# Weighted sums of two score blocks issued together in two attention layers; one layer's values by way of DRAM

## The reference, cut to what matters

```python
# causal: 16 heads of 8, 128 keys a sequence
scores = jnp.einsum('bhqd,bhkd->bhqk', q, k) * scale + alibi_bias_causal
attn = jax.nn.softmax(scores, axis=-1)
out = einsum('bhqk,bhkd->bqhd', attn, v) @ Wo.T + bo
# rotary: 16 heads of 8, 77 context rows a sequence
q, k = apply_rope(rms_norm(x @ Wq.T)), apply_rope(rms_norm(context @ Wk.T))
attn = softmax(q k^T * D ** -0.5)
out = einsum('bhts,bhsd->bthd', attn, context @ Wv.T) @ Wo.T
x = layernorm(x + out)
```

## Time and profile before

| | |
|---|---|
| median of 3 runs | 2769.44 us (2767.96 to 2771.38) |
| profiled execution | 2773.75 us |
| its span, first to last instruction | 2772.0 us |
| PE, DVE, ACT, POOL busy | 91%, 69%, 60%, 61% of the span |
| causal stage, about | 1302 to 1827 us of the span |
| rotary stage, about | 1827 to 2420 us of the span |
| L1140 transposes, both stages | x1024 each |
| L1040 sums, both stages | x2048 records each |

### The profile page before, as it was taken

The page is one execution under the profiler, slowest core; times in us unless marked ns, Lnnn a source line. Parts: engine busy times, 40 slices in busy tenths (PEclk is TensorE's granted clock), DMA queues, the critical chain, the costliest instruction groups (busy, mean ns, idle before and its releaser), DMA issues. The chain is left out here.

```text
span 2772.0 us, 61590 instructions
## 1 busy us (share of the span) xinstructions
PE 2534.0 (91%) x19168; PEld 1864.5 (67%) x19168; DVE 1904.9 (69%) x5298; ACT 1671.0 (60%) x4543; POOL 1694.9 (61%) x2110
## 2 busy tenths in 40 slices
PE   8998999999999289996999999969999999699996
PEld 6665887877877289993555555547766666458993
DVE  6884677787777355555777777765788886445655
ACT  6773666666665234444766666639888887623334
POOL 3442334555555645554888888846688887724675
PEclk9998999999999699998999999979999999899998
DMA  8932467777774122214100000000011010011336
GB/s 260 338 107 68 151 215 226 234 224 224 223 220 129 54 65 71 72 58 129 58 11 9 9 11 9 7 25 13 16 30 30 30 30 17 30 30 54 93 93 194
DMA packets 274799, 267.86 MB, mean 97 GB/s; under 512 B 30060, under 2 KB 253561, under 8 KB 274096
## 3 DMA queue, kind: packets, MB, share of 16 engines
q1 hardware_dynamic: 256912, 228.42, 27.2%
q0 software_dynamic: 17280, 34.13, 3.6%
q10 hardware_dynamic: 288, 1.38, 0.2%
HBM read 101.24 MB, written 151.85 MB: 91 GB/s over the span
## 5 line engine op out<-in xcount | busy, mean ns | idle before, releaser
L779 POOL TENSOR_TENSOR wide_probs<-wide_exps,wide_inv_sum 128x616 f32<-128x616 f32 x128 | 168.3, 1315 | 305.6 <-DVE wide_inv_sum L1580 293.0
L749 POOL TENSOR_TENSOR causal_exps<-causal_biased,causal_neg_max 128x512 f32<-128x512 f32 x256 | 262.8, 1036 | 76.4 <-DVE causal_neg_max L1594 76.2
L758 POOL DMA_INDIRECT sorted_x<-send,place_i x240 | 244.1, 1017 | 84.2 <-ACT send L1233 44.0
L1289 ACT ACTIVATE rotary_exps<-banks,rotary_neg_max 128x77 f32<-128x77 f32 x1024 | 248.7, 341 | 19.3 <-DVE rotary_neg_max L1594 19.1
L1764 POOL DMA_INDIRECT results<-gelu_tile_out,gelu_dest_i x142 | 140.1, 986 | 142.2 <-DVE gelu_tile_out L1920 120.0
L1539 DVE TENSOR_TENSOR causal_biased<-banks,regions 128x512 f32<-128x512 f32 x256 | 163.6, 680 | 80.7 <-PE banks L1115 80.4
L1764 POOL DMA_INDIRECT results<-swiglu_tile_out,swiglu_dest_i x142 | 144.6, 1019 | 116.7 <-DVE swiglu_tile_out L1915 59.4
L1833 ACT ACTIVATE gelu_hidden<-banks,gelu_slot 128x256 f32<-128x256 f32 x284 | 116.6, 470 | 159.5 <-PE banks L2010 159.4
L1258 ACT ACTIVATE causal_exps<-causal_exps 128x512 f32<-128x512 f32 x256 | 161.2, 630 | 71.4 <-POOL causal_exps L749 71.4
L1594 DVE TENSOR_REDUCE rotary_neg_max<-banks 128x4 f32<-128x308 f32 x256 | 121.7, 475 | 113.5 <-PE banks L1129 105.1
L1273 ACT ACTIVATE causal_probsT<-banks 128x512 f32<-128x512 f32 x256 | 151.6, 592 | 79.3 <-PE banks L1140 79.3
(11 more groups left out here) (385 smaller groups left out, 7018.3 us busy)
## 6 DMA issues: line engine op xcount, KB each, us to landing
v_dram<-wide_staged SPq DMA_DIRECT2D x38, 1024.0 KB, 4.4
sorted_x<-blank SPq DMA_DIRECT2D x1, 34848.0 KB, 116.8
sorted_x<-blank SPq DMA_DIRECT2D x24, 1452.0 KB, 8.7
wide_folded<-v_dram SPq DMA_DIRECT2D x128, 256.0 KB
gelu_tile_in<-sorted_x SPq DMA_DIRECT2D x71, 132.0 KB, 2.1
swiglu_tile_in<-sorted_x SPq DMA_DIRECT2D x71, 132.0 KB, 2.1
gelu_back<-results SPq DMA_DIRECT2D x16, 512.0 KB, 8.0
swiglu_back<-results SPq DMA_DIRECT2D x16, 512.0 KB, 5.4
```

The costliest lines, as they stand in the source:

```text
L749: pool.tensor_tensor(exps[:, (NU * pair.c + m) % ES], biased[:, m % BS].rearrange("p (h n) -> p h n", h=HU), neg_max[:, m % SLOTS].unsquee ...
L758: pool.indirect_dma_start(route["sorted_x"], bass.IndirectOffsetOnAxis(ap=r_place_i[:, b % 2, which, n // 2:n // 2 + 1], axis=0), send[:, ...
L779: pool.tensor_tensor(probs[:, half % SLOTS, 0:HH * NK].rearrange("p (k h) -> p h k", h=HH), exps[:, half % EB], inv_sum[:, half % SLOTS].u ...
L1289: last = act.activation(exps[:, (NU * c.c + k) % ES, h], scores[:, h * NK:(h + 1) * NK], ACT.Exp, bias=neg_max[:, k % SLOTS, h:h + 1])
```

## The change

Three things change; the wide stage is left as it was.

1. In causal, `late_sums` replaces `late_sum`: at every even k it issues the sums of two slots together, ahead of that slot's transposes, with PLAG 5 in place of 4 and four `probsT` buffers in place of two.
2. In causal, the output's way is moved: `turn_back` and `divide` from k = 4 and 6 to 5 and 6, the values' projection from k = 3 to 4, `turn_outputs` from k = 7 to k = 1 of the next step, ACT's copy from k = 0 to 2, `project_late` from k = 1 to 3 (with it the sum and statistics on DVE from 2 to 4 and the root on POOL from 3 to 5), the residual on POOL from k = 3 to 6, the norm on DVE from k = 5, 6 to 6, 7.
3. In rotary the exponentials of eight heads (two slots) are written densely, 616 columns of 77 behind one another, padded to five blocks of 128. Two transposes at the even slot and three at the odd one turn them; ACT copies 128 x 256 and 128 x 384. `dense_sum` multiplies at odd slots only: each 32-column strip holds two heads that lie in two neighbouring blocks, so 4 strips x 2 blocks = 8 matmuls (16 records) for two slots, over all 128 rows. The values must lie in the same order: ACT writes them to `v_rows` (one buffer), SP stores them with four DMAs a pair to DRAM, and loads them back five pairs behind its first role with five DMAs a pair into `v_dense`, which has two buffers. The values' projection moves from f to e (k = 7, four steps earlier), so the lead steps have it too, and ACT's copy waits until the pair before has been stored. The context ring shrinks from 8 to 4 pairs.

```diff
-    FU = {"wide": 7, "causal": 4, "rotary": 2}[kind]
+    FU = {"wide": 7, "causal": 4, "rotary": 1}[kind]
-    EARLY = 2
+    EARLY = 3
-    OT, OT_LAG = (1, 1) if kind == "causal" else (2, 0)
+    OT, OT_LAG = (1, 3) if kind == "causal" else (2, 0)
+            def store_values(pair):
+                sp.wait_ge(early_done, pair.count(EARLY, EARLY))
+                rows = ...
+                for h in range(4):
+                    sp.dma_start(rows[h], v_rows[0:NK].rearrange("k (m r) -> k m r", r=PITCH)[:, :, 64 * h:64 * h + 64]
+                                 ).then_inc(v_stored, 16)
+            def load_values(pair):
+                sp.wait_ge(v_stored, 16 * 4 * (pair.c + 1))
+                if pair.c >= 2:
+                    sp.wait_ge(pv_done, pair.back(2).count(NU, NU))
...
+            def step(f, ahead=None, pair=None, *behind):
                 if f is not None:
                     load(f)
+                if kind == "rotary" and pair is not None:
+                    store_values(pair)
+                if kind == "rotary" and behind[2] is not None:
...
+                    load_values(behind[2])
+                    if kind == "rotary" and f.c >= CTX:
+                        sp.wait_ge(early_done, f.back(CTX).count(EARLY, EARLY))
...
+            if m == 4:
+                if f.c >= 1:
+                    act.wait_ge(v_stored, 16 * 4 * f.c)
+                return act.activation(v_rows[0:NK]...[:, :, 0:D], chip.banks[0:NK, 6, 0:2 * P]..., copy)
-                    "causal": [(0, 0), (1, 0), (2, 0), (3, 1)], "rotary": [(5, 0), (7, 0)]}[kind]
-        EARLY_AT = [(0, 0), (1, 0)]
-        TLAG, PLAG, OLAG = {"wide": (4, 5, 6), "causal": (3, 4, 5), "rotary": (2, 3, 4)}[kind]
+                    "causal": [(0, 0), (1, 0), (2, 0), (4, 1)], "rotary": [(5, 0)]}[kind]
+        EARLY_AT = [(0, 0), (1, 0), (7, 0)]
+        TLAG, PLAG, OLAG = {"wide": (4, 5, 6), "causal": (3, 5, 5), "rotary": (2, 3, 4)}[kind]
+        DIVIDE_AT = (5, 6) if kind == "causal" else (4, 6)
...
+            def late_sums(pair, n):
+                b, g = n // UB, n % UB // 2
+                pe.wait_ge(probsT_done, pair.count(NU, n + 1))
...
+                for odd in range(2):
+                    for h in range(HU):
+                        strip = 272 * 2 * b + 256 * odd + 32 * (4 * g + h)
+                        last = pe.matmul(o_bank[b][32 * h:32 * h + 32, g * P:(g + 1) * P], values[:, pair.c % 2, strip:strip + 32],
+                                         probsT[:, (n - 1 + odd) % 4, h * P:(h + 1) * P], start=odd == 0, stop=odd == 1)
+                last.then_inc(pv_done, 2)
+            def dense_sum(pair, n):
...
+                    pe.wait_ge(v_loaded[s], 16 * 5 * (pair.c // 2 + 1))
+                for second in range(2):
+                    for strip in range(4):
+                        chunk = strip + second
+                        last = pe.matmul(o_bank[b][32 * strip:32 * strip + 32, g * P:(g + 1) * P],
+                                         v_dense[:, s, b, g, chunk, 32 * (strip % 2):32 * (strip % 2) + 32],
+                                         probsT[:, (NU * pair.c + n) // 2 % 2, chunk * P:(chunk + 1) * P], start=second == 0, stop=second == 1)
+                    if kind == "causal" and at is not None and k % 2 == 0:
+                        late_sums(*at)
+                            for m in range(3 if n % 2 else 2):
+                                at = (2 * (n % 2) + m) * P
+                                last = pe.transpose(p_bank[n % 2][:, m * P:(m + 1) * P], exps[:, (NU * pair.c + n) // 2 % 2, at:at + P], ident)
+                            start, columns = 2 * (n % 2) * P, (3 if n % 2 else 2) * P
+                            act.activation(probsT[:, half % 2, start:start + columns], p_bank[n % 2][:, 0:columns], ACT.Copy).then_inc(probsT_done, 1)
-                    if kind == "causal" and u is not None and k == 7:
-                        turn_outputs(u)
+                    if kind == "causal" and mine is not None and k == 1:
+                        turn_outputs(mine)
```

More of the change, by code:

```diff
@@ L438, in softmax_attention @@
         xT = sb("xT", [P, 2, 2, P])
-        if late:
+        if kind == "causal":
             values = sb("values", [P, 2, STRIPS])
+        if kind == "rotary":
+            v_rows = sb("v_rows", [P, 8 * PITCH])
+            v_dense = sb("v_dense", [P, 2, 2, 2, CHUNKS, 64])
         keys = sb("keys", [P, 2, H, 2, NK] if kind == "wide" else [P, 2, KH, NK])
-        exps = sb("exps", [P, ES, HU, NK] if late else [P, EB, HH, NK])
+        exps = sb("exps", {"wide": [P, EB, HH, NK], "causal": [P, ES, HU, NK], "rotary": [P, 2, CHUNKS * P]}[kind])
         if late:
@@ L457, in softmax_attention @@
             oT = sb("oT", [P, 2, 2, P])
-        residual = sb("residual", [P, 2, 2, P])
+        if kind != "rotary":
+            residual = sb("residual", [P, 2, 2, P])
         z = sb("z", [P, 4, 2, P])
@@ L534, in softmax_attention @@
         ready, prepared, prepared_ps, product_done = (sem(n) for n in ("ready", "prepared", "prepared_ps", "product_done"))
-        READY = {"wide": 4, "causal": 5, "rotary": 5}[kind]
+        READY = {"wide": 4, "causal": 5, "rotary": 7}[kind]
         ROOT = 3 + 3 * NEWTON
         PREPARED = {"wide": 2, "causal": 4, "rotary": 10}[kind]
+        if kind == "rotary":
+            v_stored, v_loaded = sem("v_stored"), [sem(f"v_loaded{n}") for n in range(2)]
         if kind == "wide":
@@ L673, in load @@
                         sp.dma_start(into, source).then_inc(landed, 16)
-            run_steps(sp, step, n_pairs, 3 if kind == "wide" else 1, 4)
+            run_steps(sp, step, n_pairs, {"wide": 3, "causal": 1, "rotary": 6}[kind], 4)
         def wait_loaded(engine, f):
@@ L726, in _ @@
                 pool.memset(folded[:, :, :, :, CHUNKS - 1], 0.0).then_inc(ready, 1)
-            if kind != "wide":
+            if kind == "causal":
                 pool.memset(values[:], 0.0).then_inc(ready, 1)
-            if late:
+            if kind == "rotary":
+                pool.memset(v_rows[:], 0.0).then_inc(ready, 1)
+                pool.memset(v_dense[:, :, :, :, CHUNKS - 1], 0.0).then_inc(ready, 1)
+                pool.memset(exps[:, :, HALF_ROWS:CHUNKS * P], 0.0).then_inc(ready, 1)
+                pool.wait_ge(ready, 4)
+                pool.memset(v_rows[:].rearrange("p (m w) -> p m w", w=PITCH // 4)[:, :, D:D + 1], 1.0).then_inc(ready, 1)
+            if kind == "causal":
                 pool.wait_ge(ready, 4)
@@ L787, in step @@
                         add_halves(e)
-                    if c is not None and kind != "rotary" and k == 3:
+                    if c is not None and kind != "rotary" and k == (6 if kind == "causal" else 3):
                         wait_loaded(pool, c)
@@ L1145, in step @@
                         front(f, k, 0)
-                    if late and u is not None and k in (4, 6):
-                        turn_back(u, (k - 4) // 2)
+                    if late and u is not None and k in DIVIDE_AT:
+                        turn_back(u, DIVIDE_AT.index(k))
                     at = lagged(c, u, k, PLAG)
@@ L1150, in step @@
                         weighted_sum(*at)
-                    if at is not None and late:
-                        late_sum(*at)
+                    if at is not None and kind == "rotary" and at[1] % 2 == 1:
+                        dense_sum(*at)
                     if f is not None:
@@ L1284, in step @@
                         scores = s_bank[k % 2]
-                        if before(c, k, ES) is not None:
+                        half = (NU * c.c + k) // 2
+                        if kind == "rotary" and half >= 2:
+                            act.wait_ge(probsT_ps, 2 * half - 2)
+                        if kind == "causal" and before(c, k, ES) is not None:
                             bc, bk = before(c, k, ES)
@@ L1288, in step @@
                         for h in range(HU):
-                            last = act.activation(exps[:, (NU * c.c + k) % ES, h], scores[:, h * NK:(h + 1) * NK], ACT.Exp,
-                                                  bias=neg_max[:, k % SLOTS, h:h + 1])
+                            at = (HU * (k % 2) + h) * NK
+                            into = exps[:, half % 2, at:at + NK] if kind == "rotary" else exps[:, (NU * c.c + k) % ES, h]
+                            last = act.activation(into, scores[:, h * NK:(h + 1) * NK], ACT.Exp, bias=neg_max[:, k % SLOTS, h:h + 1])
                         last.then_inc(exps_done, 1)
@@ L1637, in step @@
                             inverse_root(pair, NU * half + k)
-                    if u is not None and late and k in (4, 6):
-                        divide(u, (k - 4) // 2)
+                    if u is not None and late and k in DIVIDE_AT:
+                        divide(u, DIVIDE_AT.index(k))
             run(dve, step, STAGES)
```

102 lines of the change are left out of this document (64 added, 38 removed).

## The result

The changed kernel takes **2782.34 us** (median of six; five lie between 2777.43 and 2784.42) where the kernel before, timed beside it on the same chip, took 2771.89 (median of six): a ratio of 1.0041, interval 1.0028 to 1.0054. The sixth run of the changed kernel, in a slow state, took 7620.35 us; it is counted in the median and left out of the range and the ratio. The change makes the kernel slightly slower, by 0.4%, and 2703 with a range of 2670 to 2755 was forecast. The profiled execution took 2784.42 us, with a span of 2782.6 and a mean clock of 0.949 (before 0.957).

What follows compares the result with a forecast made beforehand. PE was taken to set the pace in both stages, and DVE in a quarter of rotary's pairs. Causal -31, rotary steady -43 and lead +8 gave -66 us from 2769.4: 2703 us, range 2670 to 2755.

Steps and rivals of the forecast that it cites:

- Causal, the other moves: Causal's copy, projection, statistics, root, residual and norm: order kept, so no cost but a little at the stage's end.
- Rival E: PE, less filled, has longer gaps and the clock dips in seven rotary windows, costing 22 us: 2725; chance 0.06.
- Causal's gain: Causal stage: PE loses 1.3 us a pair, 0.3 comes back, so -31 us; bounds -12 and -40.
- The wait of `turn_outputs`: Causal, k = 7: PE's 0.53 us wait for `divide` goes when moved two slots later, 0.5 us a pair.
- Merging: Causal's sums on PE: two blocks become one four times a pair, saving 0.2 us each, 0.8 a pair.
- The 0.3: Causal: of PE's 1.3 us a pair, 0.3 returns as transposes wait more for exponentials.
- Rotary, steady: Rotary's steady pairs: -1.8 us over some 8 unrouted, mean -1.25 over 23 routed; -43 us, bounds -15 and -62.
- PE's and ACT's terms: Rotary, a pair: 2.4 us less of PE from fewer transposes and merged sums, 1.1 less of ACT's copies.
- rival B: PE's freed time turns into waits on other engines, or merged passes follow no faster: 2745; chance 0.13.
- The values' way: Rotary's values through DRAM: store at 31 ns a packet, some 7 us, hidden below 11 us in steady steps.
- A lead step: Rotary's lead: ACT's copy waits for the previous store, about 7 us a step; +8 us, bounds +3 and +20.
- rival D: Rotary's store stalls ACT's copy at k = 7; at 75 ns a packet 2833, slower from about 62; chance 0.13.

Runs made afterwards that it cites:

- the root first: The changed kernel, with causal's root on POOL moved ahead of the subtraction in its slot 5: 2699.55 us, ratio 0.9748 to the kernel before.
- merging alone: The kernel before with causal's merged sums, values' projection at k = 4 and quotients at 5 and 6; outputs, root and norm unmoved: 2812.31 us, ratio 1.0146.
- the outputs' way alone: The kernel before with causal's output way moved as in the change and the root ahead of POOL's subtraction, sums unmerged: 2757.58 us, ratio 0.9962.

## Why the prediction was wrong

**Causal, the other moves: the step that failed.** The prediction held that copy, projection, statistics, root, residual and norm "keep their number and their order to each other, on POOL and DVE also, so they cost nothing". Number and order they keep. What it didn't look at is the distance: root to norm shrank from two slots to one, and within one slot POOL is still busy with 2 us of subtraction and key copy when DVE is through. The same wait, named with its place and its queue, should have been a rival. All that it takes was there to be read: POOL's order inside a slot from the code, 1.04 us each for subtraction and key copy from the trace of before, and the norm ahead of the biases on DVE. The price of the root's place is causal's sums with the wait less those with the root first, 513.4 - 429.3 = 84 us, and the medians of the two kernels are 83 apart. 63 of the 84 go with the wait when only the norm is moved; the other 21 come with the root first alone.

**The clock.** Rival E had the mechanism: PE waits longer, the clock falls. It put one dip of 3.2 us in seven rotary windows. It came in causal instead, in 13 of the 31 periods, 17.9 against 16.4 us: 1.5 us each, some 19 of the 84. The Trainium skill (TensorE: Matmul & The Clock Gate, HAM oscillation) tells that waits in a loop take the clock down time and again. The trace agrees in that the clock fell again and again, behind an idle time of 2.1 us. But such an idle time stands in every period and not every one was followed by a fall; with merging alone PE idled 2.0 us in each pair, and only four periods were longer (18.1 to 18.7 us for 17.1).

**Causal's gain, without that wait.** The forecast was 31; the runs give 56.4 (485.7 to 429.3). The wait of `turn_outputs` was sized right, 0.5 a pair. Merging was sized at 0.8 and gave 1.3. Its block came as forecast, 0.58 us start to start, on the timeline of PE after:

```profile
1504.60 0.64 PE L1093 MATMUL banks<-causal_probsT,causal_values 128*32 128x128 f32 x16
1505.18 0.66 PE L1216 MATMUL banks<-first,causal_exps 128*128 128x128 f32 x4
```

That is 2 x 0.36 - 0.58 = 0.14 saved inside and, as in the forecast, 0.09 outside, 0.9 a pair. What the other 0.4 of the 1.3 are was not traced. The 0.3 that were to come back as waits for exponentials did not: POOL went from 84 to 96% and PE's own share rose too. The base was read loosely as well: 15.67 is a mean over the stage with its short pairs at the end, and the steady period was 16.1.

**Rotary, steady: mis-sized.** -43 forecast, -23.3 measured. PE's and ACT's terms held. Groups after, with busy us and mean ns:

```profile
L1213 PE MATMUL banks<-first,rotary_exps 128*128 128x128 f32 x640 | 112.9, 275 | 0.0
...
L1351 ACT ACTIVATE rotary_probsT<-banks 128x384 f32<-128x384 f32 x128 | 65.5, 512 | 35.1 <-PE banks L1213 34.2
L1351 ACT ACTIVATE rotary_probsT<-banks 128x256 f32<-128x256 f32 x128 | 52.6, 411 | 1.9 <-PE banks L1213 1.7
```

640 transposes for 1024, copies of 512 and 411 ns against 0.51 and 0.42 taken. What failed is the step from prices to time. Without routing, the period of before was 15.7 with PE full, not the 16.5 of the chosen window; it is 14.45 now, -1.25 and not -1.8. (The -1.8 also has a slip: 14.1 us at a share of 95% is 14.8, not 14.7.) With routing the 23 periods have a mean of 17.2 before and 16.5 now, and the gain is 0.7 a pair, not 1.25: four engines do some 14 us of the 16.5 each, and the prediction took it that what PE sheds the pair sheds. That is rival B, for the routed pairs alone; 0.13 was too little, since the earlier trace rows showed DVE or POOL at 14.5 to 15.9 of 16.5 us there already.

**The values' way: right, and cheaper.** The lead after, on the timelines of SP and ACT (the store of the values, and the copy that waits for it), and the DMA share of a window over it:

```profile
1870.67 2.30 SPq L665 DMA_DIRECT2D v_rows<-rotary_v_rows  x4
...
1875.84 0.38 ACT L932 ACTIVATE rotary_v_rows<-banks 77x256 f32<-77x256 f32 x1 [1.94 <-DMA v_rows<-rotary_v_rows]
1881.24 0.38 ACT L932 ACTIVATE rotary_v_rows<-banks 77x256 f32<-77x256 f32 x1 [1.92 <-DMA v_rows<-rotary_v_rows]
...
1870.70:1875.80 5.10, 3.61 (x14) 2.94 (x14) 2.27 (x7) 0.97 (x2) 1.26 (x1) 0.50 0.71 163
...
  ACT rotary_v_rows L932: 5.9, 3
```

A lead step takes 5.4 us, for 3.1 before and 7 forecast. The last row is who waited for `v_rows`: three copies, 5.9 us, all in the lead, none in steady steps. So rival D is out. From the store's issue to the next copy are 5.2 us. A DMA share of 0.71 in 5.1 us is 58 us of work on 16 engines, for the store's 2464 packets and 384 of loads, 20 ns each, against 31 taken and the 62 at which the change would have lost. The Trainium skill (DMA: Bandwidth & Descriptors, Specifications) asks for 512 B a descriptor; here 256 B were cheap enough to stay hidden, at 163 GB/s.

**The sum.** Forecast -31 - 43 + 8; measured +28 (and 3 ahead of causal's first sum), -23 and +2. With the root first the same terms are -56, -23 and +3, and 2699.55 stands next to the 2703 forecast: that is luck in good part, since a miss of 25 us in causal and one of 20 in rotary cancel.

## What to carry to other kernels

When steps are moved along in-order queues, list for every producer and consumer on two engines how many slots lie between them before and after, and what stands ahead of the producer inside its slot; "the order is kept" says nothing of that. Put a short instruction that another engine waits for at the head of its slot: here 0.9 us of POOL's work in the right place decided over 83 us. A saving on the engine that is full in one window need not count whole in the next: look at every kind of pair, and at how full the other engines are there. Here 2.4 us less of PE were to give 1.8 and 1.25 us a pair, and gave 1.25 without routing and 0.7 with it.

## What was not expected of the hardware

The norm on DVE takes very different times at the same size. Its tile in the changed kernel, and with the root first:

```profile
L1658 DVE TENSOR_SCALAR X<-causal_z,causal_mean_var,causal_rstd x64: 339/796/1062, 1347.7 to 1857.7; 128x128 f32<-128x128 f32 x64
```

```profile
L1664 DVE TENSOR_SCALAR X<-causal_z,causal_mean_var,causal_rstd x64: 335/346/1250, 1340.0 to 1767.8; 128x128 f32<-128x128 f32 x64
```

A median of 796 ns for 346. The wait ahead of it is not the reason: with both norms in slot 7 it is gone, and the median is 780; with the outputs' way alone it is 794. What the timelines of POOL and DVE show is that a norm which starts beside one of POOL's instructions ends just behind it. The two norms of one pair of the changed kernel:

```profile
1517.48 1.03 POOL L790 TENSOR_TENSOR causal_exps<-causal_biased,causal_neg_max 128x512 f32<-128x512 f32 x1
1517.54 1.06 DVE L1658 TENSOR_SCALAR X<-causal_z,causal_mean_var,causal_rstd 128x128 f32<-128x128 f32 x1 [1.83 <-POOL causal_rstd L841]
...
1520.46 1.04 POOL L790 TENSOR_TENSOR causal_exps<-causal_biased,causal_neg_max 128x512 f32<-128x512 f32 x1 [1.26 <-DVE causal_neg_max L1682]
1520.79 0.79 DVE L1658 TENSOR_SCALAR X<-causal_z,causal_mean_var,causal_rstd 128x128 f32<-128x128 f32 x1
```

POOL's subtractions end at 1518.51 and 1521.50, the norms at 1518.60 and 1521.58. In the changed kernel all 49 norms that stand as rows of their own between 1340 and 1760 us end 0.07 to 0.09 us behind the end of an instruction of POOL. With the root first 29 of 60 such norms take 0.34 us; the other 31 end 0.07 to 0.10 behind one of POOL's. So the time of this norm goes by what POOL runs beside it. No run takes POOL's instruction away, so that it is the cause is inferred from these times and not shown by an experiment.
